# A two-block attention kernel: key and value biases as products of one row, and the second projection behind the first scores

## The reference

```python
# block 1: linear attention over the context
Q = elu(audio @ Wq.T + bq) + 1.0 ; K = elu(video @ Wk.T + bk) + 1.0 ; V = video @ Wv.T + bv
KV = einsum('btd,bte->bde', K, V) ; K_sum = K.sum(axis=1)
attn_out = einsum('btd,bde->bte', Q, KV) / (Q * K_sum[:, None, :] + 1e-6)
return layernorm(audio + attn_out @ Wo.T + bo, gamma, beta)
# block 2: a gated cell, run over the batches as time steps (2 here)
ft = sigmoid(xt @ wf.T + c @ uf.T + bf) ; it = sigmoid(xt @ wi.T + c @ ui.T + bi)
gt = tanh(xt @ wc.T + c @ uc.T + bc) ; c = ft * c + it * gt
h = tanh(einsum('tbi,oi->tbo', x, wo) + c_final @ uo.T + bo)
# block 3: softmax attention, 16 heads of 8, with a key mask
# block 4: 8 experts, top 2: relu(x @ W1 + b1) @ W2 + b2, weighted
```

## Time and profile before

| | |
|---|---|
| median of 3 runs | 200.93 us (199.88 to 201.11) |
| profiled execution | 200.62 us, of which span 198.8 |
| TensorE, VectorE, ScalarE, GpSimd busy | 166.6, 131.6, 107.5, 63.5 us |
| mean granted TensorE clock | 0.894 |
| HBM read | 5.37 MB, 30 GB/s over the span |

### The profile page before, as it was taken

The page is one execution under the profiler, slowest core; times in us unless marked ns, Lnnn a source line. Parts: engine busy times, 40 slices in busy tenths (PEclk is TensorE's granted clock), DMA queues, the critical chain, the costliest instruction groups (busy, mean ns, idle before and its releaser), DMA issues.

```text
span 198.8 us, 2343 instructions
## 1 busy us (share of the span) xinstructions
PE 166.6 (84%) x677; PEld 99.6 (50%) x677; DVE 131.6 (66%) x419; ACT 107.5 (54%) x192; POOL 63.5 (32%) x85
## 2 busy tenths in 40 slices
PE   0887995847955477999999997989999989999993
PEld 0451945313422243856555544435767746676781
DVE  7659797968145537887768687465676975637551
ACT  2385692635308551496775645756465446455541
POOL 7405022297771301151222002107252234243310
PEclk9999575585878588599999999999999999999998
DMA  5599500000000000000000000000000000001001
GB/s 190 99 364 253 176 0 2 0 3 2 2 0 0 2 0 0 0 0 3 0 0 0 0 3 2 0 2 3 0 0 0 0 0 3 0 0 53 2 0 53
DMA packets 4704, 6.04 MB, mean 30 GB/s; under 512 B 428, under 2 KB 3412, under 8 KB 4692
## 3 DMA queue, kind: packets, MB, share of 16 engines
q1 hardware_dynamic: 4128, 5.47, 9.2%
q10 hardware_dynamic: 564, 0.43, 0.7%
HBM read 5.37 MB, written 0.52 MB: 30 GB/s over the span
## 4 chain that ended last, share of the span: by engine, by line
PE 62%; DVE 22%; ACT 7%; issue 4%; DMA 2%; POOL 1%; ACTq 0%; DVEq 0%
PE bank L995 5%; PE bank L1027 5%; PE bank L1137 4%; PE bank L1139 3%; PE bank L1138 3%; PE bank L1120 3%; PE bank L1122 3%; PE bank L1121 3%; PE bank L1044 3%; PE bank L833 3%; PE bank L1047 3%; PE bank L946 3%; PE bank L953 2%; PE bank L1106 2%; DVE nmax L1388 2%
## 5 line engine op out<-in xcount | busy, mean ns | idle before, releaser
L1476 DVE SCALAR_TENSOR_TENSOR pair<-bank,pair 128x512 fp32r<-128x512 f32 x32 | 21.6, 690 | 19.0 <-ACT pair L791 18.9
L575 POOL TENSOR_TENSOR pair<-early,pair 128x512 fp32r<-128x512 f32 x16 | 20.5, 1286 | 39.1 <-ACT pair L784 39.1
L1388 DVE TENSOR_REDUCE nmax<-bank 128x2 f32<-128x308 f32 x64 | 27.3, 472 | 8.3 <-PE bank L995 8.1
L759 ACT ACTIVATE prob<-bank 128x512 f32<-128x512 f32 x40 | 22.9, 600 | 9.9 <-PE bank L1027 9.8
L494 POOL TENSOR_TENSOR rstd<-vare,m_half 128x4 f32<-128x4 f32 x10 | 10.4, 1039 | 38.3 <-DVE vare L1197 38.1
L791 ACT ACTIVATE pair<-bank 128x512 fp32r<-128x512 f32 x32 | 18.8, 596 | 6.1 <-PE bank L1122 4.8
L995 PE MATMUL bank<-pair,q_s 97*128 97x308 f32 x64 | 21.1, 396 | 1.1 <-DVE nmax L1388 0.5
L784 ACT ACTIVATE pair<-early 128x512 fp32r<-128x512 f32 x16 | 10.1, 632 | 21.0 <-DVE early L1472 21.0
L505 POOL TENSOR_TENSOR w_l<-w_s,w_h 128x512 fp32r<-128x512 f32 x8 | 10.8, 1351 | 26.0 <-DVE nm_part L1399 25.3
L1027 PE MATMUL bank<-q_s,pair 112*128 112x512 f32 x40 | 18.0, 459 | 0.1
L995 PEld LDWEIGHTS bank<-pair,q_s 97*128 97x128 f32 x64 | 12.6, 210 | 10.3 <-DVE nmax L1388 4.7
(11 more groups left out here) (218 smaller groups left out, 328.5 us busy)
## 6 DMA issues: line engine op xcount, KB each, us to landing
w_s<-in_w SPq DMA_DIRECT2D x1, 1024.0 KB, 7.0
prob<-in_w SPq DMA_DIRECT2D x1, 1024.0 KB, 11.7
x_t<-in_x SPq DMA_DIRECT2D x2, 256.0 KB, 3.3
wf_s<-in_w_ffn SPq DMA_DIRECT2D x1, 512.0 KB, 5.6
row<-in_rows SPq DMA_DIRECT2D x1, 260.0 KB, 4.7
wc_s<-in_w_ctx ACTq DMA_DIRECT2D x1, 256.0 KB, 4.1
out_x<-x SPq DMA_DIRECT2D x1, 256.0 KB, 2.1
out_x<-x SPq DMA_DIRECT2D x2, 128.0 KB, 1.8
```

The costliest lines, as they stand in the source:

```text
L575: pool.tensor_tensor(ec_l[:, n % NEC], ec[:, n % NEC], ec_h[:, n % NEC].bitcast(F32), ALU.subtract).then_inc(ec_lo, 1)
L759: nc.scalar.activation(prob[:, u % NPR], bank[ST[u % 3]][:], ACT.Exp).then_inc(prob_ready, 1)
L1388: dve.tensor_reduce(nmax[:, b, q, j, g:g + 2], item_bank("score", n)[:, 0:2 * TK].rearrange("p (h k) -> p h k", k=TK), AX.X, ALU.max, nega ...
L1476: dve.scalar_tensor_tensor(out=hid_l[:, g % NH], in0=bank[RING[g % 4]][:], scalar=0.0, in1=hid_h[:, g % NH].bitcast(F32), op0=ALU.max, op1 ...
```

## The change

It has six parts.

- Loading: x of batch 1 goes behind the context weights on SP's queue, the three bias rows come as one row on one partition (row_kv), and the small loads move from ScalarE's queue to SP's.
- Biases: TensorE first multiplies a column of ones with the bias row into banks 0 and 1, and keys and values accumulate on it. The rests of both batches share one tile (k0 and v0 have three tiles for four). ScalarE reads the banks (Relu for the exponential, a copy of the values). The block 3 values have a step of their own, second_values, in bank 2.
- Order: the block 3 key product goes behind the first addends, keys_picked behind gate_constants; on VectorE both keys_phi stand before the first reciprocal. k_lo moves from VectorE to GpSimd, sel's clearing too.
- GpSimd: two of the four subtractions on w1 come behind k_lo, two behind the first cell; value copies behind the second cell; all weight_lo behind nm_parts. ScalarE: one keys_of, the weight_hi and the pick copy move later.
- h: product and transposes alternate by batch; on VectorE the first ln_apply comes before the second x2.
- Scores: proj 1 goes behind the eight scores of group 0, followed by four scores of group 1 in the banks 0, 1, 6 and 4; ALONE ends at max 0, and HASTE gives the first four units one item more each.

```diff
-        ITEMS = [("turn", 0), ("proj", 0), ("turn", 1), ("proj", 1), ("query", 0), ("query", 1)]
-        ITEMS += [("score", n) for n in range(SPM)] + [("query", 2), ("max", 0)]
+        ITEMS = [("turn", 0), ("proj", 0), ("turn", 1), ("query", 0)]
+        ITEMS += [("score", n) for n in range(SPM)] + [("query", 1), ("proj", 1)]
+        SPARE = dict(zip([("score", SPM + n) for n in range(4)], (ST + (PV,))))
+        ITEMS += list(SPARE) + [("max", 0), ("query", 2)]
...
-        ALONE = ITEMS.index(("max", 0)) + 7
+        ALONE = ITEMS.index(("max", 0)) + 1
+        HASTE = 4
...
-            return min(len(ITEMS) - (u < LAST_MAX), ALONE + a * sum(PER_UNIT) + sum(PER_UNIT[:i]))
+            return min(len(ITEMS) - (u < LAST_MAX), ALONE + a * sum(PER_UNIT) + sum(PER_UNIT[:i]) + min(u + 1, HASTE))
...
-            for b in range(NB):
+            def load_x(b):
                 sp.dma_start(x_t[:, b], x[b].rearrange("(p j) d -> p j d", j=NJ)).then_inc(ld_x[b], 16)
-            sp.wait_ge(ld_ctx, 32)
-            sp.dma_start(row[:, R_BK0:N_ROWS], rows[R_BK0:N_ROWS].partition_broadcast(P)).then_inc(ld_row_k, 16)
+
+            load_x(0)
+            sp.dma_start(row_kv[:], rows[R_BK0:N_ROWS].rearrange("(o n) -> o n", o=1)).then_inc(ld_row_k, 16)
             sp.dma_start(w0_s[:], w_l0).then_inc(ld_w0, 16)
-            sp.dma_start(row[:, 0:R_BK0], rows[0:R_BK0].partition_broadcast(P)).then_inc(ld_row, 16)
+            sp.dma_start(col[:], cols).then_inc(ld_col, 16)
+            sp.wait_ge(ld_wc, 16)
+            load_x(1)
+            sp.dma_start(row[:], rows[0:R_BK0].partition_broadcast(P)).then_inc(ld_row, 16)
+            sp.dma_start(mask_u[:, :, 0:TK], mask).then_inc(ld_mask, 16)
...
+            pool.wait_ge(k_hi, 1)
+            pool.wait_ge(k_full_ready, 1)
+            pool.tensor_tensor(k_hl[:, 1], k_full, k_hl[:, 0].bitcast(F32), ALU.subtract).then_inc(k_lo, 1)
+            pool.wait_ge(den_ready, 2)
+            pool.wait_ge(ld_w1, 32)
+            w1_less_first(0)
+            w1_less_first(1)
             rstd_of(LN_R, 0)
             rstd_of(LN_X1, 0)
             rstd_of(LN_R, 1)
             rstd_of(LN_X1, 1)
-            pool.wait_ge(ld_w1, 32)
...
+            pool.wait_ge(cell_ready, 1)
+            w1_less_first(2)
+            w1_less_first(3)
...
-            pool.wait_ge(cell_ready, 1)
-            weight_lo(0)
-            weight_lo(1)
-            pool.wait_ge(cell_ready, 2)
-            weight_lo(2)
...
-                if m < 5:
-                    weight_lo(3 + m)
+                for k in ((0, 1), (2,), (3, 4), (5, 6), (7,), ())[m]:
+                    weight_lo(k)
...
-            def values_out(b):
-
-                act.wait_ge(v0_ready, b + 1)
-                nc.scalar.activation(v1[:, b, 0], bank[b][:, 2 * P:3 * P], ACT.Copy)
-                nc.scalar.activation(v1[:, b, 1], bank[2 + b][:, 2 * P:3 * P], ACT.Copy).then_inc(v1_ready, 1)
+            def keys_values(b):
+                act.wait_ge(kv_mm, b + 1)
+                nc.scalar.activation(k0_m[:, KV_OF[b]], halves(b)[:, :, 0], ACT.Relu, scale=-1.0).then_inc(k0_neg, 1)
+                nc.scalar.activation(v0[:, KV_OF[b], 0:P], halves(b)[:, :, 1], ACT.Copy).then_inc(v0_ready, 1)
...
+                if u in (10, 12):
+                    weight_hi(6 + (u - 10) // 2)
+                if u == 14:
+                    pick_copies()
...
+            def key_value_bias(b):
+
+                n = 2 - b
+                pe.wait_ge(ld_row_k, 16)
+                pe.wait_ge(ones_ready, 1)
+                rows_kv = row_kv[:, 0:2 * P].rearrange("p (o d) -> p o d", o=1).broadcast_to([1, n, 2 * P])
+                pe.matmul(bank[b][:, 0:2 * P * n], ones_r[:], rows_kv, start=True, stop=False)
+
+            def keys_values(b):
+
+                last = pe.matmul(bank[b][:, 0:2 * P], ctx_t[:, b, 0:P], wc_s[:, 0:2 * P], start=False, stop=b == 1)
+                if b == 0:
                     pe.wait_ge(ctx_rep_ready, 1)
...
+                    last = pe.matmul(bank[b][:, 2 * P:4 * P], ctx_rep[:, 0:HG].rearrange("p c k -> p (c k)"),
+                                     wc_s[:, 0:2 * P], start=False, stop=True)
+                last.then_inc(kv_mm, 1)
...
             for b in range(NB):
                 pe.matmul(bank[b][:], uo_half[:], cell[:, 1], start=False, stop=True).then_inc(h_mm, 1)
-            for b in range(NB):
                 pe.wait_ge(h_act, b + 1)
```

More of the change, by code:

```diff
@@ L110, in two_blocks @@
         col = sb("col", [P, N_COLS])
-        row = sb("row", [P, N_ROWS])
+        row = sb("row", [P, R_BK0])
+        row_kv = sb("row_kv", [1, N_ROWS - R_BK0])
         w1_s = sb("w1_s", [P, E, HC * P])
@@ L509, in add_rows @@
                 pool.tensor_tensor(dst[:, b], src[:, b], v, ALU.add).then_inc(done, 1)
+            for b in range(NB):
+                rstd_of(LN_X, b)
+            pool.memset(sel[:].bitcast(F32), 0.0).then_inc(sel_zero, 1)
             pool.wait_ge(sel_zero, 1)
@@ L707, in _ @@
                     copy_out(bank[7][:], z_f[:, 1], z_tr, 2, z_f_ready)
-                    for k in range(4):
-                        weight_hi(k)
+                    keys_of(3)
+            for k in range(2):
+                weight_hi(k)
             for b in range(NB):
@@ L914, in turn_z @@
                 transposes(bank[6 + b], z_n[:, b], z_tr)
[L916 removed]
+            key_value_bias(0)
+            key_value_bias(1)
+            pe.wait_ge(ld_ctx, 16)
+            pe.wait_ge(ld_wc, 16)
             pe.wait_ge(pad_ready, 1)
[L918 to L919 removed]
+            keys_values(0)
+            turn_a(0)
+            keys_values(1)
+            queries(0)
+            state(0)
+            state(1)
+            turn_a(1)
+            numerator(0)
+            queries(1)
+            addends(0)
             pe.wait_ge(wk_scaled, 1)
[L921 removed]
+            pe.matmul(bank[3][:, 0:NB * TKP], wc_s[:, 3 * P:4 * P], ctx_t[:], start=True, stop=True)
             pe.wait_ge(ld_col, 16)
[L923 to L935 removed]
+            pe.transpose(bank[3][0:E * HC, T - P:T], col[:, C_B1:C_B1 + E * HC], ident[:]).then_inc(k1_mm, 1)
+            second_values()
             project(0)
@@ L1332, in _ @@
             ln_apply(LN_X, 0, x_t, a_n, NJ_DVE).then_inc(a_ready, 1)
-            dve.wait_ge(ld_row_k, 16)
-            keys_values(0)
+            keys_phi(0)
+            dve.wait_ge(ld_x[1], 16)
+            ln_stats(LN_X, 1, x_t[:, 1])
+            keys_phi(1)
+            state(0)
+            constants()
             ln_apply(LN_X, 1, x_t, a_n, NJ_DVE).then_inc(a_ready, 1)
-            keys_phi(0)
             queries_phi(0)
-            state(0)
-            keys_values(1)
-            dve.wait_ge(k_hi, 1)
-            dve.scalar_tensor_tensor(out=k_hl[:, 1], in0=bank[5][:, 0:NB * TKP], scalar=bk1_q[:],
-                                     in1=k_hl[:, 0].bitcast(F32), op0=ALU.add, op1=ALU.subtract).then_inc(k_lo, 1)
+            state(1)
             reciprocal(0)
-            keys_phi(1)
             queries_phi(1)
             quotient(0)
-            state(1)
-            reciprocal(1, 0, 4)
+            reciprocal(1)
             dve.wait_ge(ld_row, 16)
```

216 lines of the change are left out of this document (103 added, 113 removed).

## The result

The changed kernel takes 194.57 us (median of 4 runs, 193.42 to 194.83), the kernel before 200.41 (4 runs, 199.25 to 201.11): a ratio of 0.9695, 95% interval 0.9651 to 0.9739. The forecast was 194.3. Now and then an execution of a kernel is slower than its others and shows a lower granted clock; the medians of this document take such executions in and the ratios leave them out, so a ratio is not the quotient of two medians. The profiled execution of the changed kernel took 194.70, of which 192.6 is span; before, 200.62 and 198.8.

A forecast was written before the change was run, and what follows sets the result against it. TensorE, whose clock falls after holes so each is paid twice, and a relay of waits up to the first score bound the kernel; terms summed to -6.6, 200.62 to 194.0, plus 0.3 for the median: 194.3 us, range 190.0 to 199.5.

The forecast's parts named there:

- front: Up to the first gate product: reciprocals sooner, but ScalarE's keys wait for later selections; +0.6 us, range -1.6 to +4.4.
- first cell, VectorE's pieces: First cell: q_e, a_n and y_t no longer slowed by GpSimd's subtractions, 3.1 less; net -2.8 us after turn_z(1).
- second y_t: Second cell: y_t no longer runs beside GpSimd's first weight_lo, which moves behind nm_parts; -0.9 us.
- order of the h products: After the second cell: batch 0's transposes no longer wait for batch 1's product, starting at 60.5, not 61.1; -0.6 us.
- second projection behind the scores: Batch 1's transposes, projection and copies no longer precede the first score, 11.5 after x2(0) instead of 12.6; -1.1 us.
- filling the hole before the exponents: TensorE's gap after the first scores takes query(1), project(1) and four scores; -1.0 us (-0.6 to -1.6).
- clock: TensorE half-rate stretches in cells and scores may go as holes shrink; a third of 4.5 counted, -1.5 us (0 to -4.5).
- ScalarE's pieces in units 10 to 14: Two weight_hi and the pick copy added to ScalarE in the score stage cost +0.7 us (0.3 to 1.0).
- rival (a): TensorE's clock holds in both places, cells and scores, and the front gains: 188.7 to 192 us; chance 0.13.
- (b): The keys hang: half rate through the selections, front +3.3, clock saves nothing: 198.5 us (197 to 199.5); chance 0.14.
- (c): Nothing gets free ahead of the reciprocals: front +4.4, no clock gain, 199.9 us; chance 0.09.
- (d): Slower by TensorE's clock alone, thin places each costing a half-rate stretch: 203 to 205 us; chance 0.08.

The follow-up runs named there:

- e1: The changed kernel unaltered, timed again beside other edits: 194.57 us, ratio 0.9667 to the kernel before.
- e7: The changed kernel with ScalarE's last two weight_hi and its pick copy moved back ahead of the scores' stage: 193.89 us, ratio 0.9656.
- e2: The kernel before with only the changed kernel's GpSimd order put in: 194.03 us, ratio 0.9653.
- e9: The changed kernel with GpSimd's four w1 subtractions back in one go in the middle of the first cell: 197.87 us, ratio 0.9879.
- e3: The changed kernel with the kernel before's TensorE order up to the exponents, no scores ahead and haste 0: 195.30 us, ratio 0.9699.
- e5: The changed kernel with unread TensorE products added around the h products, x2 transposes and first query projection: 192.65 us, ratio 0.9637.
- e6: The changed kernel with the key selections moved back ahead of the first block's first projection: 195.97 us, ratio 0.9770.
- e12: The changed kernel with haste 3, unread TensorE products in front and later, keys_of(1) behind ScalarE's normalisation, keys_of(2) later still: 190.86 us, ratio 0.9512.
- e10: The changed kernel with the kernel before's front (loading, biases, order), all else changed: 193.37 us, ratio 0.9666.

## Why the prediction was right

The forecast was 194.3; it came to 194.57. The cause that it named for its largest term was right. That the total came within 0.3 us is luck in part: two misses of over 1 us the wrong way cancel against larger gains in the cells, most of them the clock's. Effects on the profiled time, a minus being faster; the measured column is the table of leads above, and adds up to the 6.2 us of the span (the time of the profiled execution moved by 5.9, as 0.3 more lies outside the span, which the forecast had unchanged):

| term | forecast | measured |
|---|---|---|
| front | +0.6 | +0.5 (e1: +0.7) |
| first cell, VectorE's pieces | -2.8 | -3.3 |
| second y_t | -0.9 | -1.0 |
| order of the h products | -0.6 | -1.1, from the clock and not from the order (below) |
| second projection behind the scores | -1.1 | -0.7 |
| filling the hole before the exponents | -1.0 | +0.7 |
| clock | -1.5 | -2.9 (0.95 before the tanh, 1.91 in L1006; e1: -1.7) |
| ScalarE's pieces in units 10 to 14 | +0.7 | 0.1 (e7), within the next row |
| behind the first exponent product, none on record | 0 | +1.6 (1.0 of it in this execution alone) |

**The cells** are the change. The step by which q_e (1.14), two a_n pieces (2.50) and the first y_t (1.69) are slow for the four subtractions beside them named the cause, and e2 and e9 show it from both sides: GpSimd's order put into the kernel before gives 7.0 us, where the whole change gives 6.5 in the same set, and the four subtractions put back into the changed kernel take 3.3 (4.2 by the ratios). So GpSimd's order is the whole measured gain, and the other parts together show none. e9 shows it within one cell, for q_e and a_n lie beside the subtractions and are slow, y_t starts behind them and is not. The Trainium skill, page "SBUF — State Buffer", section "Who interferes with whom", says that a VectorE instruction with two SBUF inputs contends with a GpSimd instruction that reads SBUF, and not with one that only writes it. Here q_e went from 0.69 to 1.60, and the clearing of sel, which only writes, ran from 13.36 in the first profile beside a_n pieces that took 0.62 for two: the traces agree on both. (Beside GpSimd's power on 128 x 4, which reads too, the a_n pieces of the earlier trace rows took 0.62 for two as well.)

```profile
13.36 0.95 POOL L530 MEMSET sel<- 128x1028 f32 x1
...
13.49 0.62 DVE L1259 SCALAR_TENSOR_TENSOR a_n<-x_t,mv,rstd 128x128 f32<-128x128 f32 x2
```

The 0.5 us more than forecast is q_e at 0.70 for 0.76, and turn_z(1) (42.58, 0.66), which ends with y_t and does not stick out by 0.3.

**The order of the h products** failed as a term, though its row looks better than forecast. The step by which the transposes began only when both products were done, at 61.1, and could begin at 60.5, when the tanh was there, is read from a stretch at half rate. At full rate e2, with the old order, and e1, with the new one, take the same 2.64 us from the h product to x2(0); the first profile took 3.09, as its clock fell to 0.50 at 53. So at full rate the order brings nothing that shows, and the 1.1 is one more part of what the clock gave.

**The clock** was the right kind of term: a third of 4.5 was counted, the whole of L953's (4.68 to 2.78) came, and in this one execution 0.95 more in the gates, which came back to 5.47 in e1. The two holes were not alike. The one before L953 shrank from 3.6 to 1.4 us and the clock held; the one before the exponents was filled, but with work at half rate, since the clock had fallen by 60 already, behind a stretch in which TensorE was busy for less than half the time (4.47 of 10 us in e1). So rival (a) came true in the first place and not in the second. What was said against it, that the clock fell after every hole of over 1.5 us, does not hold in the changed kernel: TensorE stood for 1.58 us ahead of L933 at 30.85, and the window of 31 to 32 still shows 1.00.

**The hole before the exponents** is the step that failed most: "The first exponent product comes 1.4 to 2.4 sooner", for the hole that is filled, less 0.8 of work that is owed. No price was put on the clock at which the work in the hole would run. All of it ran at 1.2 GHz in the first profile: the eight scores took 2.95 for 2.52 before, the projection (L1031 x2) 1.71, the four scores ahead 1.96, and the first exponent product came 7.82 behind the first score, where it came 7.09 behind it before. e3 gives both score-order terms as 1.2 together at the end of the profile, for 2.1 on record, with 2.0 from the projection (1.1 on record) and -0.3 from the filled hole; e5 shows the clock as part of the reason. The kernel before took 26.66 us from x2(0) to the first product with the values, the changed kernel 26.92: what the new order gains there, the clock takes.

**Behind the exponents** the prediction put nothing, since "what is saved earlier moves the end one for one". In the first profile 1.6 of the lead went there, in e1 0.6 (6.76 at the first exponent product, 74.72): TensorE is not full all the way, it waits for VectorE's maxima at 107 and 113.

**ScalarE's pieces** found free time: the profile of e7 shows 0.1 for 0.7. ScalarE, busy for 78% there, had room for three pieces for which nobody waits.

**The front** was right in sum and in its mechanism (ScalarE directly behind keys_of(1), no wait for mean_rstd). The second reciprocal came at 21.57 and not 20.6; at full rate at 15 to 18 (e6) it is 20.72. The +0.6 was a middle between a gain at full rate and a loss at half; it came out since the half-rate stretch lay earlier, at 15 to 18, and the selections ended at 29.3, 0.5 past the 28.8 that would lose nothing. What the new front wins on VectorE it does not deliver, as the keys' chain on ScalarE ends last; e12 shortens that, and the next chain takes its place.

The other rivals: (b) did not come, the selections ended at 29.3 and the clock was up there; (c) did not come: the reciprocals were 0.4 and 0.9 sooner and the front lost 0.5 and not 4.4, though (c) is right in that the front brings nothing (e10); (d) did not come, the mean clock is 0.92.

**What stays open:** why e6's other executions are 2 us slower than its profile, whether the new front costs 0.7 or nothing, what makes the haste cost more in the medians (0.9) than in the profile (0.3), if it does, and how large the gain of the new score order is in the times.

## What to carry to other kernels

Before pricing a reordering on the busiest engine, look at what runs beside the slow instructions of the engines that are on the chain: here a few GpSimd pieces, put elsewhere in that one engine's list, were worth as much as the whole change. Price work that moves into a hole at the clock of that place: what keeps TensorE busy just ahead of it counts for as much as the hole (products that nobody reads, with haste 3, brought about 3 us more: ratio 0.9667 to 0.9526). A term read from a trace at half rate can be gone once another part of the change brings the clock back, as the order of the h products was. And a lead made at one batch's product, 3.2 us in e12, is worth little when the other batch's chain is next.

## What the runs showed of the hardware

- One execution of the changed kernel differs from another by whole stretches of TensorE's clock: the gates took 4.30 in the first profile and 5.47 in e1, at spans that both read 192.6. A term of under 1 us read from a single profile is not safe.
- A wait of 2.9 us on TensorE (e9, to 45.86) was paid with 0.8 in the products behind it, the clock being up again some 3 us later; the hole of 3.6 us before L953 cost 1.9.
- VectorE's reciprocal (3.35 for 128 x 512) took 3.34 with GpSimd's additions beside it, 3.35 without and 3.35 with two weight subtractions beside it (e1), where q_e and a_n more than doubled beside the same subtractions.
